# A tenth of the masks of a top-32 attention moved from VectorE to ScalarE and GpSimd

## The reference

```python
scores = jnp.einsum('bhsd,bhnd->bhsn', Q, K) / SCALE
topk_scores, topk_indices = jax.lax.top_k(scores, 32)
sparse_weights = jax.nn.softmax(topk_scores, axis=-1)
sel_V = jnp.take_along_axis(V[:, :, None, :, :], topk_indices[..., None], axis=3)
context = jnp.einsum('bhsk,bhskd->bhsd', sparse_weights, sel_V)
return context @ Wo.T + bo
```

## Time and profile before

| what | value |
|---|---|
| time of the kernel, median of 3 runs | 9104.57 us (9097.82 to 9106.29) |
| profiled execution: its own time | 9101.82 us |
| its span in the profile | 9100.0 us |
| mean granted clock of TensorE | 0.811 |
| this stage's first Exp, and its last division | 5174.18 and 6113.04 us |

### The profile page before, as it was taken

How to read it: one execution, slowest core, us unless ns; L and a number is a source line. 1 busy time by engine, 2 the same in 40 slices (tenths; PEclk the granted TensorE clock), 3 DMA queues, 4 the chain that set the end, 5 groups by cost and what they waited for, 6 DMA issues and landing times. The chain is left out here.

```text
span 9100.0 us, 105883 instructions
## 1 busy us (share of the span) xinstructions
PE 5934.6 (65%) x35333; PEld 1798.9 (20%) x35333; DVE 7073.8 (78%) x14504; ACT 4930.2 (54%) x5960; POOL 663.5 (7%) x323
## 2 busy tenths in 40 slices
PE   0435888864888854444244477767777776588887
PEld 0111111120111111111011011114444443111113
DVE  0449999638999748899988799986766674999963
ACT  0112777821777844444244499984544443277782
POOL 0000000000000000000000000005433342000000
PEclk9766999985999965555555699998888887699998
DMA  0440000021000000000000100000000001000001
GB/s 25 148 149 18 15 4 13 1 66 42 7 10 15 1 19 10 9 8 8 4 8 8 44 15 15 3 12 15 13 13 13 13 8 30 24 15 2 15 1 42
DMA packets 152746, 200.72 MB, mean 22 GB/s; under 512 B 12689, under 2 KB 134845, under 8 KB 150838
## 3 DMA queue, kind: packets, MB, share of 16 engines
q1 hardware_dynamic: 152182, 193.97, 7.6%
HBM read 130.67 MB, written 68.28 MB: 22 GB/s over the span
## 5 line engine op out<-in xcount | busy, mean ns | idle before, releaser
L1043 DVE TENSOR_REDUCE a_partial<-a_row 128x1 f32<-128x494 f32 x4992 | 3022.3, 665 | 192.6 <-PE a_row L923 125.9
L1009 ACT ACTIVATE a_prob<-a_score 128x1024 f32<-128x1024 f32 x2448 | 2360.6, 1021 | 605.3 <-PE a_score L936 605.1
L923 PE MATMUL a_row<-a_kg,a_qn 54*128 54x494 bf16 x4992 | 1027.4, 408 | 741.6 <-DVE a_partial L1043 659.9
L541 ACT COPY m_rows<-m_score 128x1536 f32<-128x1536 f32 (+1 forms) x640 | 760.8, 1250 | 1030.1 <-PE m_score L520 913.1
L602 DVE MAX8 m_cand<-m_rows 128x8 f32<-128x192 f32 x4352 | 1221.9, 344 | 103.7 <-issue 55.8
L948 PE MATMUL a_acc<-a_prob,a_v_all 128*9 128x512 f32 x9792 | 1282.6, 596 | 1.7 <-ACT a_prob L1009 1.4
L520 PE MATMUL m_score<-m_kb,m_qb 54*128 54x512 bf16 (+1 forms) x1664 | 766.0, 608 | 315.7 <-ACT m_rows L541 244.9
L816 DVE SCALAR_TENSOR_TENSOR a_prob<-a_score,a_prob 128x1024 f32<-128x1024 f32 x816 | 924.5, 1211 | 36.4 <-ACT a_prob L792 36.4
L792 ACT ACTIVATE a_prob<-a_score,a_lower 128x1024 f32<-128x1024 f32 x816 | 865.9, 1111 | 66.0 <-PE a_score L735 14.7
L936 PE MATMUL a_score<-a_qb,a_kg 54*128 54x512 bf16 x4896 | 760.6, 379 | 34.7 <-ACT a_prob L1009 20.7
L923 PEld LDWEIGHTS a_row<-a_kg,a_qn 54*128 54x128 bf16 x4992 | 242.1, 94 | 2336.1 <-DVE a_partial L1043 2231.2
(11 more groups left out here) (314 smaller groups left out, 6030.7 us busy)
## 6 DMA issues: line engine op xcount, KB each, us to landing
a_kg<-kst SPq DMA_DIRECT2D x64, 688.5 KB
kst<-kv_parts SPq DMA_DIRECT2D x68, 576.0 KB, 5.9
vst<-kv_va SPq DMA_DIRECT2D x68, 216.0 KB, 4.2
a_v_all<-vst SPq DMA_DIRECT2D x4, 3672.0 KB, 24.4
e_cb<-comb SPq DMA_DIRECT2D x25, 512.0 KB
m_kb<-kst SPq DMA_DIRECT2D x16, 688.5 KB
qst<-q_parts SPq DMA_DIRECT2D x4, 1536.0 KB
a_qn<-qst SPq DMA_DIRECT2D x96, 54.0 KB
```

Source lines behind the costliest of these rows:

```text
L541: act.copy(rows[i][:, c * CH:c * CH + n], score[(i * NCH + c) % 2][:, 0:n]).then_inc(copied, 1)
L923: pe.matmul(row[(use + half) % 3][:, 0:CW], qn[u % 2][rows, pair, i * P:(i + 1) * P], kg[u // NQC % 2][rows, pair, c * CW:(c + 1) * CW], s ...
L1009: act.activation(prob[tile % PROBS][:, pair, :, :], score[use % 2][:, :, :], ACT.Exp).then_inc(slot_out, 1)
L1043: dve.tensor_reduce(partial[:, u % 2, 2 * item + half, c:c + 1], row[use % 3][:, 0:CW], AX, ALU.max).then_inc(reduced, 1)
```

## The change

Three constants and one path change in `attend_to_top`; nothing else in the program does.

- Every tenth slot (n = 2, 12, 22, ... 812; always the first pair of its tile) is left out of VectorE's list. ScalarE, right behind the Exp of that slot, copies its scores from PSUM into one of two new SBUF buffers, `kept_score`. GpSimd turns the copy into zeros and ones in place (`>= 0`), waits for itself, and multiplies the probabilities by it. The score slot is free when ScalarE's copy is done.
- The sums come two tiles behind instead of one, and wait for VectorE's masks and, where the tile has such a slot, for GpSimd's.
- There are four probability buffers instead of three, and ScalarE's copy of the sums of a unit moves from tile 1 to tile 2.

```diff
-    PROBS = 3
+    PROBS = 4
     HEADS_AT = 3
+    POOLED = 10
...
+        kept_score = [m.sb(f"kept_score{i}", [P, 2, QC]) for i in range(2)]
...
+        def by_pool(n):
+            return n % POOLED == 2
+
+        def pool_uses(n):
+            return (n + POOLED - 2) // POOLED
+
+        def dve_uses(n):
+            return n + 1 - pool_uses(n)
...
-                if n >= SLOTS:
-                    pe.wait_ge(kept, n - SLOTS + 1)
+                if n >= SLOTS and by_pool(n - SLOTS):
+                    pe.wait_ge(score_copied, pool_uses(n - SLOTS))
+                elif n >= SLOTS:
+                    pe.wait_ge(kept, dve_uses(n - SLOTS))
...
-                pe.wait_ge(kept, 2 * tile + 2)
+                pe.wait_ge(kept, dve_uses(2 * tile + 1))
+                if by_pool(2 * tile):
+                    pe.wait_ge(pool_kept, pool_uses(2 * tile))
...
-                if tile:
-                    sums(tile - 1)
+                if tile >= 2:
+                    sums(tile - 2)
...
+            sums(TILES - 2)
             sums(TILES - 1)
...
+                    n = 2 * tile + pair
+                    if by_pool(n):
+                        turn = pool_uses(n) - 1
+                        if turn >= 2:
+                            act.wait_ge(pool_kept, turn - 1)
+                        act.copy(kept_score[turn % 2][:, :, :], score[n % SLOTS][:, :, :]).then_inc(score_copied, 1)
-                if tile % KT == 1 and tile > KT:
+                if tile % KT == 2 and tile > KT:
                     keep_sums(tile // KT - 1)
...
+        @block.gpsimd
+        def _(pool):
+            for n in range(2 * TILES):
+                if by_pool(n):
+                    turn, share = pool_uses(n) - 1, prob[n // 2 % PROBS][:, n % 2, :, :]
+                    pool.wait_ge(score_copied, turn + 1)
+                    pool.tensor_scalar(kept_score[turn % 2][:, :, :], kept_score[turn % 2][:, :, :], 0.0, None,
+                                       ALU.is_ge).then_inc(pool_marked, 1)
+                    pool.wait_ge(pool_marked, turn + 1)
+                    pool.tensor_tensor(share, share, kept_score[turn % 2][:, :, :], ALU.mult).then_inc(pool_kept, 1)
...
+                    if by_pool(n):
+                        continue
                     dve.wait_ge(exped, n + 1)
```

More of the change, by code:

```diff
@@ L693, in attend_to_top @@
         scored, exped, kept, summed = m.sem("scored"), m.sem("exped"), m.sem("kept"), m.sem("summed")
+        score_copied, pool_marked, pool_kept = m.sem("score_copied"), m.sem("pool_marked"), m.sem("pool_kept")
         acc_zeroed, ob_ready, turned, rden_ready, att_ready = (
```

## The result

The changed kernel takes 9151.4 us (median of 5 runs, 9150.19 to 9155.35) against 9106.3 for the kernel before in the same comparison: 45 us slower, ratio 1.0052 with a 95% interval of 1.0039 to 1.0065. The forecast was 9124.2, its range ended at 9150. The direction was right, the size was not: somewhat more than twice the forecast loss, and just outside the range. The profiled execution has a span of 9148.3 us.

What follows compares the result with a forecast made beforehand. VectorE was taken to pace the `attend_to_top` stage, ScalarE close behind. Longer rounds +21.1, masks after waits +0.8 and the start −2.3 gave +19.6 us on 9104.6: 9124.2 us, range 9094 to 9150.

Steps and rivals of the forecast that it cites:

- GpSimd's two operations: Comparison and multiplication of a copied tile on GpSimd: 4.0 us (3.5 to 4.8), done before that tile's sums, no cost.
- the price: Time of GpSimd's operations: comparison 1.5 us (bounds 1.09 and 2.35), 0.1 wait, multiplication 2.35.
- the slack: Time GpSimd has before the copied tile's sums: 4.8 us, and 0.39 more before mask 7 would be late.
- the second rival: GpSimd is late: every 0.1 us past about 5.1 adds 0.1 a round, 8 us in all; about 9200; chance 0.11.
- The round of 11.57 us: Ten slots of the attention loop, from one copied slot's Exp to the next: 11.57 us against 11.31, 0.26 longer.
- my sum: All terms of the forecast together: 21.1 + 0.8 − 2.3 = +19.6 us.
- 21.1 + 0.8: Cost of 81 rounds: 0.26 us each for the longer round, 0.01 each for masks starting after a wait.
- The start: At the stage's start, later sums let slots 5 and 6 finish before `v_all` lands: −2.3 us.
- Masks beside GpSimd: VectorE's masks running while GpSimd works keep their length: nothing put in.
- the third rival: Masks are stretched beside GpSimd, three to four a round by 1.07 us each: +263 us, about 9390; chance 0.03.
- the first: ScalarE alone paces the stage, VectorE's standing absorbed, round 11.0 us: −24.8 us, 9080; chance 0.11.
- the fourth: The change moves less than counted, round within 0.02 us of its old length: about 9104; chance 0.10.

Runs made afterwards that it cites:

- e1: The changed kernel with the sums three tiles late instead of two and five probability buffers instead of four: 9129.3 us, ratio 1.0026 to the kernel before.
- e2: The changed kernel without GpSimd's comparison, so that probabilities are multiplied by raw scores: 9124.7 us, ratio 1.0024 to the kernel before.
- e3: The kernel before with only the sums two tiles late, four probability buffers and the sums' copy at tile 2: 9097.3 us, ratio 0.9992.
- e6: Against the changed kernel, every fourth slot gives 256 of its 1024 columns to ScalarE and GpSimd; VectorE masks the rest after the copy: 9062.1 us.
- e8: The changed kernel with GpSimd's comparison run twice, the second time on zeros and ones: 9506.8 us in one run.

## Why the prediction was wrong, and where it was right

**The step that failed** is "GpSimd's two operations ... 4.0 us (3.5 to 4.8). Not late." It failed twice, in the price and in the slack.

*The price.* The comparison takes 2.77 us, not 1.5, and more than the two-input operation that I had set as its upper end. With 0.08 between them and 2.38 for the multiplication GpSimd needs 5.23 us, 0.4 more than the 4.8 it has. The error was to treat it as a bound that a comparison costs between a cast (1.09) and a two-input operation (2.35); it was an analogy. So the second rival, that GpSimd is late, came true. A gap of 0.3 us between the end of a guessed range and the 5.1 from which the second rival decides deserved much more than a chance of 0.11.

*The slack.* The moment at which the sums would stand was right (6.94 against 6.9). But the sum allowed 0.39 us more "before it costs anything", counted to mask 7 alone, and by the second rival's rule the true 5.23 would have cost 0.13 a round, 11 us in all. Measured are 11.90 − 11.60 = 0.30 and 23 us. The sums start 0.15 after the multiplication's end (5366.17 to 5366.32), which was not counted. And what comes due first is not mask 7 but ScalarE's own chain: in e1 the Exp of slot 7 starts 8.33 us after the copied slot's (5355.07 to 5363.40), and since three more starts at 1.0 lead to the next copied Exp, it can't start later than 11.60 − 3.00 = 8.60 without lengthening the round. That is a slack of 0.27. The sums were 0.55 late, and the difference is the round's growth. The size of the miss is worked out; that the lateness caused it is shown by e1 and e2: 23 us of the stage, 20 to 25 of the time, each against the kernel before in its own comparison.

**The round of 11.57 us** was right in its mechanism and short by 0.03: 11.60 with GpSimd out of the way. The one link that differs in the rows is Exp to mask behind the copy, 1.17 us in e1 (5356.96 to 5358.13) and 1.19 in the changed kernel (5360.72 to 5361.91) instead of 1.14, since that Exp is longer (1.15 in the changed kernel, instead of 1.11). The stage of e1 is 23.0 us longer than before, where my sum had 19.6. Without e3's 2.7 the rounds cost 25.7, where I had 21.1 + 0.8: this term was undersized by some 4 us; had GpSimd been in time, the forecast of 9124 would have stood (e1 9129, e2 9125).

**The start** was forecast to give 2.3 us. e3's stage is 2.7 shorter, but that is near it by luck: 1.3 came at the start and 1.4 at the changes of unit, for which the forecast had nothing. **Masks beside GpSimd** kept their length, mean 1.216 against 1.211, as forecast; the third rival falls. So does the first, since no engine was full, and the fourth, since the round stayed 0.3 longer with GpSimd in time. The Trainium skill (SBUF — State Buffer, Who interferes with whom) has a VectorE instruction with at most one SBUF input not contend with GpSimd, and these masks agree.

**The terms of the measured loss**, in the stage: +46.2 = 23.2 for the lateness (changed kernel less e1), −2.7 for the later sums (e3), and the remaining 25.7, 0.31 a round, for 82 copies that VectorE has to wait out. Outside this distance the stage's end takes 3.2 us more than before, for which the forecast had nothing. The third tile of e1 doesn't help there, 8.8 us pass again from the last Exp to the last division (6132.6 to 6141.34); without the comparison, in e2, it is 5.5 as before (6128.4 to 6133.87).

## What to carry to other kernels

Handing an instruction from a full engine to an idle one helps only as far as the buffers between them let one run ahead: with three slots ScalarE's lead over VectorE was 0.4 to 0.5 us, so a copy of 0.9 us cost more than the mask of 1.13 us saved, and copies of 0.25 us left VectorE hardly any idle time. Work through one period of the loop from start to start before adding up busy times, and cut what is moved into pieces smaller than the lead. For work off the path, compute its deadline along every engine that waits behind it, and if the price of an operation there has no row of its own, take the chance that it is missed seriously.

## What the runs showed of the hardware that was not expected

- GpSimd's comparison of 128x1024 f32 with a constant, in place in SBUF, took 2767 ns, longer than its multiplication of two such tensors, 2367. For 256 columns they took 0.85 and 0.73 us on average (e6). The Trainium skill (GPSIMD Engine Reference, 3.1 Elementwise — side-by-side cycle accounting) gives about 1.8 cycles an element as the best case of a tight loop, an estimate of 1.54 us for this comparison; the measurement decides.
- Exps that run just behind the copy took 1.15 us instead of 1.11, and their starts stayed 1.0 apart. GpSimd's work beside them isn't needed for that: in e2 the fourth Exp behind the copy starts 0.4 us after GpSimd's multiplication has ended and is 1.15 us long too. What lengthens them wasn't tried.
- A stall that left TensorE busy 65% instead of 72% of the stage came with a granted clock of 0.81 instead of 0.99, and the run took some 127 us more than the stall's own expected price (e8).
